# Splitting weights in place and forming fused products inside the first turn; next x loaded into a second tile; turns laid out anew

## The reference

```python
# attention: q, k, v = h@Wq, h@Wk, h@Wv (biases in layer 0)
scores = where(mask, q @ k.T * scale, -big)
out = softmax(scores) @ v;  y = out @ Wo + bo
# L2, for each head
Wh = h @ W.T + bW;  e = Wh @ attn
A = tanh(where(adj, e @ Wh.T, 0));  hp = relu(A @ Wh)
ha = cat(hp) @ A_w.T;  hf = h @ fc_w.T
coeff = sigmoid(hf @ g1_w.T + ha @ g2_w.T + gbias)
out = hf * coeff + ha * (1 - coeff)
```

## Time and profile before

| | us |
|---|---|
| median of 3 runs | 2044.17 (2043.49 to 2051.04) |
| profiled execution | 2054.13 |
| its span, first to last instruction | 2052.2 |
| PE, weight loads, DVE, ACT, POOL busy | 1863.7, 1632.1, 1401.5, 953.2, 184.6 |
| mean granted clock of PE | 0.966 of 2.4 GHz |

### The profile page before, as it was taken

One profiled execution on the slowest core, in us unless ns is written; L12 is line 12 of the kernel. 1 busy time (PEld: TensorE's weight loads), 2 busy tenths in 40 slices (PEclk: granted clock), 3 DMA queues, 4 the chain that ended last, 5 costly groups with the idle time before them and its releaser, 6 DMA issues.

```text
span 2052.2 us, 58068 instructions
## 1 busy us (share of the span) xinstructions
PE 1863.7 (91%) x23607; PEld 1632.1 (80%) x23607; DVE 1401.5 (68%) x3776; ACT 953.2 (46%) x3578; POOL 184.6 (9%) x297
## 2 busy tenths in 40 slices
PE   7699999999999999999999999999999999999997
PEld 6588778788778788778788878888878878877876
DVE  4466776767777677676777676777667677677763
ACT  3344544444544544454544554444454454454452
POOL 0000011000011001001001001100001100001100
PEclk8699999999999999999999999999999999999998
DMA  5000000000000000000000000000000000000000
GB/s 190 1 3 13 13 12 12 3 13 13 13 11 13 13 3 13 13 13 11 13 3 13 13 13 11 13 3 13 13 13 11 13 3 13 13 13 11 12 7 6
DMA packets 36532, 30.62 MB, mean 15 GB/s; under 512 B 11568, under 2 KB 36144, under 8 KB 36336
## 3 DMA queue, kind: packets, MB, share of 16 engines
q1 hardware_dynamic: 36336, 27.48, 4.4%
HBM read 19.08 MB, written 8.39 MB: 13 GB/s over the span
## 4 chain that ended last, share of the span: by engine, by line
PE 43%; issue 29%; DVE 12%; ACT 6%; DMA 5%; POOL 4%; SPq 0%; POOLq 0%; DVEq 0%
PE ps L453 38%; DMA x<-x 4%; ACT probs L819 4%; POOL small L432 3%; PE ps L613 2%; DVE small L957 2%; PE ps L539 2%; DVE xn L972 2%; DVE small L963 1%; DVE probs L1047 1%; POOL row_terms L436 1%; ACT probsT L826 1%; DVE f L1117 1%; ACT hT L794 1%; DVE xn L1057 1%
## 5 line engine op out<-in xcount | busy, mean ns | idle before, releaser
L453 PE MATMUL ps<-hT,w_hi 128*128 128x256 f32 x2560 | 501.3, 288 | 9.6 <-ACT hT L794 6.4
L453 PE MATMUL ps<-w_hi,hT 128*128 128x256 f32 (+1 forms) x1536 | 432.4, 346 | 0.0
L453 PEld LDWEIGHTS ps<-hT,w_hi 128*128 128x128 f32 x2560 | 412.4, 191 | 24.7 <-ACT hT L794 11.1
L819 ACT ACTIVATE probs<-probs,small 128x64 f32<-128x64 f32 x1024 | 341.8, 338 | 90.5 <-DVE small L1037 90.2
L453 PE MATMUL ps<-hT,w_lo 128*128 128x256 f32 x1280 | 334.6, 283 | 0.0
L432 POOL TENSOR_TENSOR small<-small,consts 128x1 f32<-128x1 f32 x256 | 149.6, 584 | 1789.6 <-DVE small L965 1789.6
L453 PEld LDWEIGHTS ps<-w_hi,hT 128*128 128x128 f32 x1536 | 268.0, 188 | 44.2 <-DVE wh L1089 10.1
L453 PE MATMUL ps<-w_lo,hT 128*128 128x256 f32 (+1 forms) x768 | 249.7, 337 | 0.0
L453 PEld LDWEIGHTS ps<-hT,w_lo 128*128 128x128 f32 x1280 | 244.4, 191 | 0.0
L794 ACT ACTIVATE hT<-ps 128x256 fp32r<-128x256 f32 x256 | 88.0, 383 | 311.1 <-PE ps L539 311.1
L453 PE MATMUL ps<-w_hi,oT 128*128 128x256 f32 x768 | 194.5, 326 | 23.9 <-DVE oT L888 22.9
(11 more groups left out here) (114 smaller groups left out, 3325.7 us busy)
## 6 DMA issues: line engine op xcount, KB each, us to landing
raw_mats<-mats SPq DMA_DIRECT2D x8, 1024.0 KB, 10.6
x<-x SPq DMA_DIRECT2D x32, 256.0 KB, 2.8
out<-xn SPq DMA_DIRECT2D x32, 256.0 KB, 2.9
adj<-adjq SPq DMA_DIRECT2D x64, 16.0 KB, 2.1
adjT<-adjt SPq DMA_DIRECT2D x64, 8.0 KB, 2.4
raw_consts<-board_consts SPq DMA_DIRECT2D x1, 451.5 KB, 2.8
w_bias<-rows SPq DMA_DIRECT2D x1, 256.0 KB, 4.5
bias_cols<-cols SPq DMA_DIRECT2D x1, 6.0 KB, 2.6
```

What stands on the lines that cost most here:

```text
L453: return nc.tensor.matmul(o, lhsT, rhs, start=start, stop=stop, skip_group_check=True)
L819: last = fn(p, p, ACT.Exp, bias=ROWMAX[s][:, row:row + 1], accum_out=ROWSUM[s][:, row:row + 1])
```

## The change

- The matrices are loaded into `RAWLO`, a view of the bytes of `WLO` (four W and one other into `RAWHI`, a view of `WHI`), and split there: ACT copies them to `WHI`, DVE writes the difference over the source.
- Of the setup only the first two splits stay ahead of the turns. Everything else goes into `prepare`, which `passes` calls after named steps of slot 0 in its first turn: on PE the bias rows after `v0.1`; the output bias, the one-column vectors and T1 after `scores0`; G of two heads each after `out0.1` and `scores1`; the gate's product after `out1.1`. ACT and DVE have their copies, splits and small vectors at steps to match. PE has separate waits for the splits of each layer.
- SP loads x of slot 0 ahead of the matrices, each group of matrices has a semaphore of its own, and x of slot 1 comes after the matrices.
- x is loaded into a new tile `XP`, once `ha` of the slot's L2 is done. Statistics and norm of layer 0 read `XP`; `bias` writes `X` from it and waits there for the store. `out` of attention 3 writes `X`, and that is stored. `norm` has no wait for the store.
- `bias` comes after `mask` and `max` in all attentions.
- All four lists of `ORDER` are new; the lag is 59 for PE (56), 62 for ACT (58), 64 for DVE and POOL as before. Where the new x enters, PE's lists read (A is slot 0, B slot 1):

```diff
+IN_L0, IN_ATT, IN_W, IN_FC, IN_FCN, IN_G, IN_L1, IN_WT, IN_A, IN_L3 = range(10)
+LOADS = {IN_L0: (0, 0, 4), IN_ATT: (M_G, R_ATT, 4), IN_FC: (M_FG, R_FCT, 1), IN_G: (M_FG + 1, R_G1T, 2),
+         IN_L1: (4, 4, 4), IN_WT: (M_W, R_WT, 4), IN_A: (M_A, R_AW, 4), IN_L3: (8, 8, 4)}
+
+SPLITS = [(IN_L0, 0, 2), (IN_L0, 2, 2), (IN_L1, 4, 4), (IN_WT, M_W, 4), (IN_A, M_A, 4), (IN_FC, M_FG, 1),
+          (IN_G, M_G2, 1), (IN_L3, 8, 4)]
...
+            softmax += [("bias", a, 0)] + [("exp", a, u) for u in us[:half + 1]] + [("soft", a, u) for u in us[:half]]
             softmax += [("pt", a, 0)] + [("exp", a, u) for u in us[half + 1:]] + [("heads", a, 0)]
             softmax += [("soft", a, u) for u in us[half:]] + [("pt", a, 1), ("pv", a, 0), ("heads", a, 1), ("pv", a, 1)]
-            return (norm_steps(a) + [("bias", a, 0)] + [(k, a, i) for k in ("q", "k", "v") for i in range(2)]
+            return (norm_steps(a) + [(k, a, i) for k in ("q", "k", "v") for i in range(2)]
...
                     step(0, STEPS[k], now)
+                    if first and prepare is not None:
+                        prepare(*STEPS[k])
...
-            for n in (4, 3, 5, 0, 1, 2, 6, 7):
-                sp.dma_start(RAWM[:, 4 * n:4 * n + 4, :, :],
-                             mats_in[4 * n:4 * n + 4, :, :].rearrange("m (c p) o -> p m c o", p=P)
-                             ).then_inc(raw_sems[max(n - 2, 0)], 16)
-
             def load_x(s, g):
-                sp.dma_start(X[s][:, :].rearrange("p (t d) -> p t d", t=TT), x_v[:, g, :, :]).then_inc(S[s]["x_in"], 16)
+                sp.dma_start(XP[s][:, :].rearrange("p (t d) -> p t d", t=TT), x_v[:, g, :, :]).then_inc(S[s]["x_in"], 16)
 
             def load_adj(s, g):
                 for half in range(2):
...
+            def load_mats(n, o, r, k):
+                sp.dma_start(o, mats_in[r:r + k, :, :].rearrange("m (c p) o -> p m c o", p=P)).then_inc(raw[n], 16)
+            def load_raw(n):
+                load_mats(n, RAW[n], *LOADS[n][1:])
+            load_x(0, 0)
+            load_raw(IN_L0)
+            load_adj(0, 0)
+            load_raw(IN_L1)
+            load_raw(IN_ATT)
+            load_mats(IN_W, WNAT, R_WNAT, H2)
+            load_mats(IN_FCN, RAWHI[:, M_FG + 1:M_FG + 2, :, :], R_FCNAT, 1)
+            load_raw(IN_G)
+            load_raw(IN_WT)
+            load_raw(IN_A)
+            load_raw(IN_FC)
+            load_raw(IN_L3)
+            load_x(1, 1)
+            load_adj(1, 1)
...
-                sp.wait_ge(S[s]["res"], now.six[5])
-                if gnext is not None:
+                    sp.wait_ge(S[s]["ha_ps"], now.two[1])
                     alone(sp)
                     load_x(s, gnext)
-                sp.dma_start(out_v[:, g, :, :], XN[s][:, :].rearrange("p (t d) -> p t d", t=TT)
+                sp.wait_ge(S[s]["res"], now.six[5])
+                sp.dma_start(out_v[:, g, :, :], X[s][:, :].rearrange("p (t d) -> p t d", t=TT)
                              ).then_inc(S[s]["stored"], 16)
...
+                elif (k, a, i) == ("scores", 0, 0):
+                    pe.wait_ge(setup["bw_sb"], 1)
+                    pe.wait_ge(setup["bv"], 1)
+                    for n in range(3):
+                        o = PS[:, 6 + n // 2, n % 2 * D:n % 2 * D + D]
+                        last = mm(o, SELR[:, 1, :], RAWROWS[:, (n + 1) * D:(n + 1) * D + D], True, n > 0)
+                        if n == 0:
+                            for c in range(DC):
+                                mm(o, BVB[:, c, :], WHI[:, 3, c, :].bitcast(F32), False, False)
+                                mm(o, BVB[:, c, :], WLO[:, 3, c, :].bitcast(F32), False, c == DC - 1)
...
+                    pe.wait_ge(raw[IN_ATT], 16)
+                    for h in range(H2):
+                        for oc in range(DC):
+                            for c in range(DC):
+                                last = mm(PS[:, 4, oc * H2 + h:oc * H2 + h + 1], ATTN[:, h, c, oc * P:oc * P + P],
+                                          bcol[:, h, c:c + 1], c == 0, c == DC - 1)
+                    last.then_inc(setup["vec_ps"], 1)
+                    pe.wait_ge(raw[IN_W], 16)
+                    for h in range(H2):
+                        if h == 0:
+                            pe.wait_ge(setup["bv"], 1)
+                        elif h == 1:
+                            pe.wait_ge(setup["vec_sb"], 1)
+                        else:
+                            pe.wait_ge(setup["t1_sb"], h - 1)
+                        for oc in range(DC):
+                            for c in range(DC):
+                                last = mm(PS[:, 5 - h % 2, oc * D:oc * D + D], ATTN[:, h, c, oc * P:oc * P + P],
+                                          WNAT[:, h, c, :], c == 0, c == DC - 1)
+                        last.then_inc(setup["t1_ps"], 1)
...
+                elif (k, a, i) in (("out", 0, 1), ("scores", 1, 0)):
+                    first = 2 * a
+                    pe.wait_ge(setup["bo_sb"], 1)
+                    for h in range(first, first + 2):
+                        pe.wait_ge(setup["t1_sb"], max(h + 1, 3 + h % 2))
+                        if h >= 2:
+                            pe.wait_ge(setup["g_lo"], h - 1)
+                        at = 0
+                        for ic in range(DC):
+                            for c in range(DC):
+                                at = ic * H2 + h
+                                mm(PS[:, 6, at:at + 1], T1[:, h, c, ic * P:ic * P + P], bcol[:, h, c:c + 1],
+                                   c == 0, c == DC - 1)
+                                mm(PS[:, 7, at:at + 1], WNAT[:, h, c, ic * P:ic * P + P], A1[:, c, h:h + 1],
+                                   c == 0, c == DC - 1)
+                        for ic in range(DC):
+                            for c in range(DC):
+                                last = mm(PS[:, 5 - h % 2, ic * D:ic * D + D], WNAT[:, h, c, ic * P:ic * P + P],
+                                          T1[:, h, c, :], c == 0, c == DC - 1)
+                        last.then_inc(setup["g_ps"], 1)
...
+                elif (k, a, i) == ("turn", L2, 1):
+                    pe.wait_ge(setup["w_lo"], 7)
+                    pe.wait_ge(setup["g_lo"], H2 + 1)
+                    pe.wait_ge(setup["vec_sb"], 3)
+                    pe.wait_ge(setup["rows"], 5)
+                elif (k, a, i) == ("turn", 0, 1):
+                    pe.wait_ge(setup["w_lo"], 1)
+                elif (k, a, i) == ("k", 0, 1):
+                    pe.wait_ge(setup["w_lo"], 2)
+                elif (k, a, i) == ("turn", 1, 1):
+                    pe.wait_ge(setup["w_lo"], 3)
+                elif (k, a, i) == ("turn", 2, 1):
+                    pe.wait_ge(setup["w_lo"], 8)
...
+            def prepare(k, a, i):
+                if (k, a, i) == ("turn", 0, 1):
+                    split_hi(2)
...
+                elif (k, a) == ("exp", 0) and i[0] == 0:
+                    act.wait_ge(setup["bo_ps"], 1)
+                    fn(BOB[:, 0:2, :], PS[:, 6, :], ACT.Copy)
+                    fn(BOB[:, 2, :], PS[:, 7, 0:D], ACT.Copy).then_inc(setup["bo_sb"], 1)
+                elif (k, a) == ("exp", 0) and i[0] in (1, 2):
+                    t1_out(2 * i[0] - 2)
+                    t1_out(2 * i[0] - 1)
+                elif (k, a, i) == ("out", 0, 1):
+                    g_hi(0)
+                    g_hi(1)
+                elif (k, a, i) == ("turn", 1, 1):
+                    split_hi(3)
+                elif (k, a, i) == ("q", 1, 1):
+                    split_hi(4)
+                elif (k, a, i) == ("v", 1, 1):
+                    split_hi(5)
+                    split_hi(6)
+                elif (k, a) == ("exp", 1) and i == units(1)[1]:
+                    g_hi(2)
+                    g_hi(3)
+                elif (k, a, i) == ("out", 1, 1):
+                    g_hi(4)
+                elif (k, a, i) == ("e", L2, 3):
+                    split_hi(7)
...
+            def prepare(k, a, i):
+                if (k, a, i) == ("norm", 0, 1):
+                    split_lo(0)
+                    split_lo(1)
+                elif (k, a, i) == ("turn", 0, 1):
+                    bias_rows()
+                elif (k, a, i) == ("k", 0, 1):
+                    split_lo(2)
...
+                elif (k, a) == ("max", 0) and i[0] == 1:
+                    dve.wait_ge(setup["vec_ps"], 1)
+                    nc.vector.tensor_copy(A1[:, :, :], PS[:, 4, 0:DC * H2]).then_inc(setup["vec_sb"], 1)
+                elif (k, a) == ("max", 0) and i[0] == 3:
+                    dve.wait_ge(setup["bo_sb"], 1)
+                elif (k, a, i) == ("norm", 1, 1):
+                    g_lo(0)
+                    g_lo(1)
+                elif (k, a, i) == ("turn", 1, 1):
+                    split_lo(3)
+                elif (k, a, i) == ("k", 1, 1):
+                    split_lo(4)
+                elif (k, a, i) == ("v", 1, 1):
+                    split_lo(5)
+                    split_lo(6)
```

(52 more changed lines are left out.)

232 lines of the change are left out of this document (103 added, 129 removed), and 38 rows, old and new, of the table ORDER.

## The result

| | before | after |
|---|---|---|
| median of 20 runs each, us | 2046.99 (2039.59 to 2053.93) | 2031.1 (2027.6 to 2043.8) |
| ratio to before, with its 95% interval | | 0.9936 (0.9923 to 0.9948) |
| span of the profiled execution, us | 2052.2 | 2027.9 |
| slot 0's first output issued, us | 164.83 | 141.32 |
| mean of the 14 turns that follow, us | 122.21 | 122.24 |

39 were forecast. The first output is some 6 us earlier than the forecast had it (147 us); the steady turn, which was to lose 1.5 us, did not move.

What follows compares the result with a forecast made beforehand. PE, busy 91% of the span, was taken to bound the kernel. From the median of 2044.17 us, 17 us for the start and 22 for the early load came off: 2005 us; own range 1985 to 2022, wider range 1965 to 2036.

Steps and rivals of the forecast that it cites:

- The start: Slot 0's first turn: setup moved inside it leaves 10 us ahead, plus 7 from PE's clock: 17 us gained, 4 to 25.
- 2.0 MB in by about 8 us: Start: constants, x and the first layer's matrices loaded by then, at 256 GB/s; first mask at about 22.4 us.
- the row of 44.70 us: Trace of before, 44.70 to 45.12 us: one-column products at half clock, taken against G blocks gaining 1 or 2 us.
- The early load: Steady turns: x loaded early takes 2.6 us from each slot's cycle; PE gets 1.5 a turn, times 15, 22 us.
- rival 1: Steady turns: the chain limits and each turn gets the whole wait: 39 + 17 = 56 us, 1988 us; chance 0.22.
- 0.57 us is what PE loses there: PE's stop before the transposes at the load, cited for rival 2, that the load was hidden.
- the estimate of 2.3 us that the gaps could take: Steady turn: three `e` steps fill PE gaps of 0.95 and 0.81 us, and the 0.57 at the load goes.
- PE has only 9.2 us to give: Steady turn: PE idles 9.2 of 122.2 us, most of it elsewhere; the argument against rival 1.
- nothing, or 0.68 us a turn where DVE is late: Cost of moving the bias add from before K to after the maxima, where ACT's exponentials run.
- The new wait for the store: DVE's store wait moves from norm to bias add, 11 us of steps later: cost nothing, unless the store were later.
- Rival 3: Tails: PE waits for the transposed probabilities' copy, clock under 0.97; 2 us a turn lost, 2057 us; chance 0.10.
- Rival 2: Steady turns: the load was hidden, PE stops as before, and only the start is gained: 2027 us; chance 0.22.

Runs made afterwards that it cites:

- e6: e5 with x loaded late again, so of the change only the new start is left: 2031.15 us, 0.9929 of before.
- e7: The kernel before with only the bias add moved late, behind the maxima: 2078.72 us, 1.0155 of before.
- e13: The kernel before with only the other slot's `r` put ahead of the statistics on DVE: 2030.92 us, 0.9909 of before.
- e11: e5 with half of the fused products left out (T1, G and their one-column vectors; gate's product whole): 1984.7 us, 0.9683 of before.
- e5: e2 with the bias add back in its old place (new start, early x, old lists): 1998.82 us, 0.9756 of before.
- e1: The changed kernel run once more, unaltered, as control: 2031.89 us, 0.9921 of before.
- e3: e2 with x loaded late again (old lists, late bias add, new start): 2057.79 us, 1.0049 of before.
- e8: The changed kernel with two of the other slot's `e` steps put back ahead of each slot's first transposes on PE: 2026.26 us, 0.9895 of before.
- e9: The changed kernel with only the bias add back in its old place, new lists kept: 2041.48 us, 0.9973 of before.
- e10: e6 with the other slot's `r` ahead of the waiting statistics on DVE at both slots' starts: 2010.77 us, 0.982 of before.
- e12: e5 with the other slot's `r` ahead of the statistics on DVE: 1999.8 us, 0.9771 of before.
- e2: The changed kernel with the old lists and lags put back (new start, early x, late bias add kept): 2023.7 us, 0.9887 of before.
- e4: The changed kernel with x loaded late again, new lists kept: 2178.78 us, 1.0633 of before.

## Why the prediction was right or wrong

**The start: right.** 17 us forecast, 15 measured with nothing else of the change but the tiles that x and the output use (e6, 9 to 20 by its interval). The profiles show the first output 22 us earlier (143.05 in e6, 141.32 in after); of the 7 us between, before's profiled execution, 7 us above its median, can be the cause; its turns don't tell where. One profile is a rough measure here: the first output comes at 161.01 to 165.97 us in the three kernels with the old start (before, e7, e13), and at 138.58 to 149.40 in the eleven with the whole new one. Within it two terms were off and cancelled. The matrices were later than thought (first mask 24.86 instead of 22.4 us): "2.0 MB in by about 8 us" was wrong, ACT got the first of them at 11.95 us:

```profile
11.95 2.00 ACT L824 ACTIVATE w_hi<-raw_lo 128x1024 fp32r<-128x1024 f32 x2 [3.86 <-DMA raw_lo<-mats]
```

The products were cheaper in after: T1 took 7.15 us, not the 10.03 of the earlier trace rows, and two heads' G with their one-column products stand from 45.35 to 52.59 us, 7.2 us, not 9.0. That is the clock, and not every profile has it (below). That they take their whole length on slot 0's chain is borne out by e11.

**The clock at the products: the kind of product does not decide it.** The prediction let the row of 44.70 us speak, one-column products at the half clock with no gap. Windows of after, of e5, and of e11 twice, all within or around G's products:

```profile
47.00:49.20 2.20, 2.20 (x14) 1.99 (x14) 1.15 (x5) 0.00 (x0) 1.20 (x2) 1.00 0.01 4
```

```profile
44.00:48.00 4.00, 4.00 (x21) 4.00 (x20) 2.01 (x7) 0.00 (x0) 0.47 (x1) 0.51 0.00 0
```

```profile
40.00:43.00 3.00, 3.00 (x11) 2.73 (x12) 2.09 (x8) 0.00 (x0) 0.89 (x2) 0.50 0.01 3
...
54.20:56.00 1.80, 1.80 (x15) 1.71 (x13) 1.80 (x2) 0.18 (x1) 0.00 (x0) 1.00 0.03 9
```

PE is busy all the time in each; the clock is 2.4 GHz in the first and last, 1.2 GHz in the two between. Nor do the instructions decide it: the first two heads' G, the same in all kernels that form them whole inside the turn, take 7.2 to 7.4 us in the profiles of after, e1, e3, e6, e8, e9, e10 and e12, and 13.65 us in e2, e4 and e5, whose first outputs come at 147.87 to 149.40 us against 138.58 to 143.69 in the eight. e5 and e12 differ only in the place of `r` on DVE and lie on either side; each kernel has one profile, so whether one kernel can do both was not seen. By the Trainium skill, "TensorE: Matmul & The Clock Gate", section "What's actually happening", the gate follows how busy PE has been. The first and the last agree; the two between, busy without a gap and at half clock, do not, if busy is read from this column. What released the clock in the eight and not in the three was not settled. The forecast's own line, that these products stay slow, did not hold for after; it did for e5.

**The early load: right sign, term too small.** 22 us forecast, 32 measured (e6 to e5): 2.2 us a turn, still inside the forecast's 1.2 to 2.3, and 2.54 by the profiles, which is the size of rival 1, "each turn gets the whole wait". The step that failed here is "0.57 us is what PE loses there" as the measure of the cost, and with it the estimate of 2.3 us that the gaps could take. The wait on DVE held up `r` of the other slot (20 of the 32 us, e10), and PE paid for that later and elsewhere. This error alone would have left the kernel faster than forecast. Nor is PE's busy time a fixed amount to be packed: in the turn of e5 PE is busy 111.45 us, in e6 112.80, for the same instructions, so that 1.35 of the 2.54 us come out of what the page counts as busy. Mean over the 14 turns, e5:

```profile
sum 1675.21, PE 1560.27 PEld 1378.86 DVE 1204.16 ACT 817.82 POOL 160.28; mean PE 111.45 PEld 98.49 DVE 86.01 ACT 58.42 POOL 11.45
```

The Trainium skill, "Trainium Kernel Development and Optimization", in its opening note on reading a trace, calls matmul busy time a bad metric; the trace agrees: "PE has only 9.2 us to give" was read from that column, and it spoke against the rival whose size the load turned out to have.

**The bias add: the failed step of the sum.** The prediction put it at "nothing, or 0.68 us a turn where DVE is late". In the old lists it costs 25 us (e5 to e2) and 32 us in before (e7), 1.8 us a turn. Two errors are in the sentence. It names ACT's exponentials as the cover, but DVE itself is the busy engine there, with `wh` of the other slot and the scaling behind the add. And it prices one add; the change moves three in each slot, six a turn, 4.1 us of DVE work put into softmaxes, of which a bit under half shows. The new wait for the store, which the prediction had looked at closely, is not among the waits of after: it cost nothing that shows.

**The new lists: right that they are a risk, wrong in how.** Rival 3 had them lose 2 us a turn in the tail, with the clock down in it. They cost 0.65 us a turn on top of the late bias (e2 to e1, 8 us). The clock did fall, 0.962 of after against 0.978 of e2, and 8 of the 14 turns of after are under the 0.97 that the prediction named as the rival's sign, against one of before. The stop that the rival named, for the copy of the transposed probabilities, did grow as well, but by 0.4 to 0.5 us a turn. It has the releaser "issue" in these waits of PE in the 14 turns, before and then after (of the 39.0, 37.3 us are this stop, against 31.4 in e2):

```profile
PE ps L453 <- issue: 30.8, 63, 1.1
```

```profile
PE ps L484 <- issue: 39.0, 66, 1.5
```

The other waits changed places: in the 14 turns of e2 PE stands 33.0 us for the scaled probabilities and 38 for norms and `oT`, in after none and 79.

**The sum as measured:** start 15, early load 32, bias add minus 25, new lists minus 8: 14 us, the change's 13 to 16. The terms hold in this order only: with the new lists before the late bias they are minus 43 (e5 to e9) and plus 10 (e9 to e1), so the zero for the bias add and the order laid out around it failed together. Rival 2's number, 2027 us, came nearest, but by another mechanism: the load was not hidden, its gain was eaten by two other parts of the same change. The forecast's own range, 1985 to 2022, does not hold the time; the wider range does.

The best complete kernel of these is e5, new start and early x in the old lists with the old bias: 1998.82 us, 2.4% under before; e12 equals it.

## What to carry to other kernels

The price of a wait on an in-order engine is not only the stop that the bounding engine shows there, but also what stands behind the wait and could have run (here 20 of 32 us): read the rows after it before costing it, and first try to let them pass. A step moved "under" another engine's work needs a gap on its own engine, or an order laid out for it (in the new lists the late bias lost nothing), and every copy of it per turn counts. Where a change joins several parts, a zero in the sum is as much a claim as the large terms, and the first experiment should undo it.

## What the runs showed of the hardware

Two norm steps of DVE, the same operation on the same tile shape, differ by almost a factor of three. In before, both norm steps on DVE, and POOL's row that runs beside the second:

```profile
965.14 0.41 DVE L972 TENSOR_SCALAR xn<-x,small 128x256 f32<-128x256 f32 x1
966.00 1.13 DVE L972 TENSOR_SCALAR xn<-x,small 128x256 f32<-128x256 f32 x1 [0.44 <-POOL small L432]
...
965.94 1.04 POOL L436 TENSOR_TENSOR row_terms<-rs,consts 128x512 fp32r<-128x512 f32 x1
```

The slow one lies under POOL's product of 128x512 from its start to that product's end (966.98 us), so contention between the two is likely; it was not tried alone. It is not what the early load changes: the norms of layer 0 last 782 ns on average in e6, 757 in e10 and 784 in e5. The other surprise is the clock at G's products, above: the same products with PE busy throughout at 2.4 GHz in eight profiles and at 1.2 in three, a factor of two on work that slot 0's chain waits for.
